# The second layer of a pair kernel in a written-out order, with the last chunk's banks and the last norm dealt out anew

## What is computed

```python
# layer one, per token (s, r)
x  = layernorm(pair) * ln1_w + ln1_b
left  = sigmoid(x @ left1) * (x @ left2)
right = sigmoid(x @ right1) * (x @ right2)
p  = layernorm(einsum('nsre,nkre->nske', left, right)) * ln2_w + ln2_b
x1 = pair + (p @ out_w) * sigmoid(x @ gate)
# layer two
l    = x1 @ (W_left + W_eq) + biases
rsum = sum of (x1 @ W_right + b_right) over one token axis
o    = l * rsum * sigmoid(x1 @ W_gate + b_gate)
out  = layernorm(o @ W_out + b_out + x1) * ln_scale + ln_bias
```

## Time and profile before

| what | before |
|---|---|
| median of three runs | 112.12 us |
| profiled execution | 112.37 us |
| its span, first to last instruction | 110.6 us |
| TensorE busy | 94.1 us (85%) |
| VectorE busy | 75.8 us (69%) |
| ScalarE busy | 66.4 us (60%) |
| GpSimd busy | 62.3 us (56%) |
| granted TensorE clock, mean | 0.968 |

### The profile page before, as it was taken

How to read it: one execution, slowest core, us unless ns; L and a number is a source line. 1 busy time by engine, 2 the same in 40 slices (tenths; PEclk the granted TensorE clock), 3 DMA queues, 4 the chain that set the end, 5 groups by cost and what they waited for, 6 DMA issues and landing times. The chain is left out here.

```text
span 110.6 us, 1889 instructions
## 1 busy us (share of the span) xinstructions
PE 94.1 (85%) x600; PEld 73.9 (67%) x600; DVE 75.8 (69%) x284; ACT 66.4 (60%) x110; POOL 62.3 (56%) x78
## 2 busy tenths in 40 slices
PE   1997889999999899999979999999999996499100
PEld 1994568667787899354536789777887885399000
DVE  1474799957879500989957599699789954983500
ACT  0633987977774366885699445982896499221000
POOL 5059954999910310055289595587865491799300
PEclk9999999999999999999999999999999999959985
DMA  3999990000000000000000000000032006029996
GB/s 59 190 152 143 147 134 21 0 0 0 0 0 3 6 0 0 0 0 3 0 0 0 9 0 0 0 0 6 0 55 40 0 0 95 0 41 146 145 146 101
DMA packets 33546, 4.54 MB, mean 41 GB/s; under 512 B 33408, under 2 KB 33536, under 8 KB 33536
## 3 DMA queue, kind: packets, MB, share of 16 engines
q1 hardware_dynamic: 31776, 4.03, 29.7%
q10 hardware_dynamic: 1760, 0.38, 1.8%
HBM read 2.31 MB, written 2.10 MB: 40 GB/s over the span
## 5 line engine op out<-in xcount | busy, mean ns | idle before, releaser
L596 DVE TENSOR_TENSOR lr<-bank,sig_lr 128x512 f32<-128x512 f32 x16 | 15.9, 1043 | 3.9 <-ACT sig_lr L431 3.9
L817 PE MATMUL bank<-lr_blk,xnT 64*128 64x256 f32 x128 | 16.5, 392 | 1.2 <-ACT xnT L421 0.7
L354 POOL TENSOR_TENSOR t_tok<-p_sb,rstd 128x512 f32<-128x512 f32 x7 | 10.2, 1461 | 11.8 <-DVE rstd L666 11.8
L362 POOL TENSOR_TENSOR x_low<-x1T,x_high 128x512 fp32r<-128x512 f32 x8 | 10.3, 1293 | 7.5 <-ACT x_high L501 7.5
L817 PEld LDWEIGHTS bank<-lr_blk,xnT 64*128 64x128 f32 x128 | 11.7, 186 | 4.2 <-issue 2.1
L660 DVE BATCH_NORM_STATS2 stats<-p_sb 128x6 f32<-128x64 f32 x64 | 8.5, 213 | 7.0 <-ACT p_sb L465 7.0
L370 POOL TENSOR_TENSOR oT<-o_a,rsum 128x512 f32<-128x512 f32 x8 | 8.7, 1088 | 6.4 <-DVE o_a L706 4.3
L431 ACT ACTIVATE sig_lr<-bank 128x512 f32<-128x512 f32 x16 | 9.6, 598 | 3.7 <-PE bank L817 3.6
L978 PE MATMUL bank<-wout_blk,oT 128*128 128x128 f32 x64 | 9.4, 293 | 2.2 <-POOL oT L370 2.2
L978 PEld LDWEIGHTS bank<-wout_blk,oT 128*128 128x128 f32 x64 | 8.5, 201 | 4.0 <-POOL oT L370 3.2
L501 ACT ACTIVATE x_high<-x1T 128x512 fp32r<-128x512 f32 x8 | 5.0, 626 | 8.5 <-DVE x1T L697 8.4
(11 more groups left out here) (104 smaller groups left out, 202.3 us busy)
## 6 DMA issues: line engine op xcount, KB each, us to landing
x_tok<-in_x SPq DMA_DIRECT2D x14, 128.0 KB, 4.2
out<-sq SPq DMA_DIRECT2D x7, 256.0 KB, 3.4
x_tok<-in_x SPq DMA_DIRECT2D x3, 64.0 KB, 3.0
w_rep<-in_weights ACTq DMA_DIRECT2D x4, 45.1 KB, 3.1
out<-sq ACTq DMA_DIRECT2D x1, 128.0 KB, 4.0
out<-sq SPq DMA_DIRECT2D x1, 128.0 KB, 4.5
x_tok<-in_x ACTq DMA_DIRECT2D x1, 64.0 KB, 2.7
row_rep<-in_rows SPq DMA_DIRECT2D x1, 32.0 KB, 4.2
```

The source lines that it names most:

```text
L354: nc.gpsimd.tensor_tensor(place(t_tok[:, c % 2], 0, SPC), even_first(p_sb[:, :, s]), even_first(rstd[:, 1:2, s]).to_broadcast([P, 2, SPC / ...
L362: nc.gpsimd.tensor_tensor(x1_low[:, c % 2], x1T[:, c % 3], x1_high[:, c % 2], ALU.subtract).then_inc(x1_low_ready, 1)
L596: nc.vector.tensor_tensor(lr[:, :, s].rearrange("p f s -> p s f"), src[:, :, 2 * CH:4 * CH], sig_lr[:, j % 3].rearrange("p (s f) -> p s f" ...
L817: last = nc.tensor.matmul(dst, xnT[half, c, k * P:(k + 1) * P], lr_blk[half].rearrange("p g m c -> p g (m c)"), start=True, stop=True, ski ...
```

## The change

Layer two is written out call by call on all four engines. Up to the fourth chunk the order is nearly that of the loops. Later chunks are interleaved more finely: the gate's and left side's matmuls are split into a part before and a part after `x1_low` is needed, `project_q`, `transpose_x` and `transpose_t` run ahead, and `residual0` is parted into `residual0` (`u`) and `add_x` (the four additions). Further:

- Chunks 0 and 7 are not split: `gate_whole` and `left_whole` are one float32 matmul each on `x1T`; `high1` and `low1` of the two go. Chunk 7 uses banks 0 and 1 for them, and its result and that of chunk 6 go to banks G and XT, so that `centre_y` of both needn't wait for the banks Y.
- `project_scaled`, `normalise3` and the scaled weights go. Chunks 6 and 7 take the way of the others.
- GpSimd makes `scale3` of 0, 1 and 4 and `bias3` of 0, 1, 4, 5, 6; VectorE `scale3` of 2, 3, 5, 6, `bias3` of 2 and 3, and all of chunk 7.
- The roots are taken in five groups, not six; stores are issued in the order 0, 2, 1, 3, 4, 5, 6.

```diff
-ROOTS3 = [(0, 1), (1, 3), (3, 5), (5, 6), (6, 7), (7, 8)]
+ROOTS3 = [(0, 1), (1, 3), (3, 6), (6, 7), (7, 8)]
+WHOLE = (0, 7)
+POOL_SCALES = [0, 1, 4]
+POOL_BIASES = [0, 1, 4, 5, 6]
+DVE_SCALES = [2, 3, 5, 6]
+DVE_BIASES = [2, 3]
+STORES = [0, 2, 1, 3, 4, 5, 6]
+        LAST_G, LAST_L = TT, Q
+        Y_BANK = [Y, Y + 1, Y, Y + 1, Y, Y + 1, XT, G]
...
 # GpSimd; before: times_right, low1, times_right, normalise2, bias3 by a loop
+            pool.wait_ge(r_in, 16)
+            normalise2(1); normalise2(2); normalise2(3); low1(1); normalise2(4)
+            times_right(0); low1(2); times_right(1); normalise2(5); low1(3)
+            normalise2(6); scale3(0); times_right(2); low1(4); bias3(0)
+            times_right(3); normalise2(7); low1(5); times_right(4)
+            scale3(1); bias3(1); low1(6); times_right(5); times_right(6)
+            scale3(4); bias3(4); times_right(7); bias3(5); bias3(6)
...
 # ScalarE, from the second root of layer two on
+            root2_of(3); root3_of(0); evacuate_y(1); evacuate_tT(5)
+            sigmoid_table(); gate1(3); high1(4); evacuate_tT(6); evacuate_y(2)
+            high1(5); gate1(4); root3_of(1); evacuate_y(3)
+            sigmoid_table(); gate1(5); evacuate_tT(7); high1(6); evacuate_y(4)
+            gate1(6); evacuate_y(5); root3_of(2)
+            sigmoid_table(); gate1(7); evacuate_y(6); root3_of(3)
+            evacuate_y(7); root3_of(4)
...
 # VectorE, from chunk 4 on
+            residual0(4); add_x(4); sums_of_right(1); residual0(5); gated1(3)
+            add_x(5); weigh3(1); variance3(1); weigh3(2); gated1(4)
+            variance3(2); sums_of_right(2); residual0(6); inverse3(1); add_x(6)
+            scale3(2); weigh3(3); bias3(2); gated1(5); weigh3(4); residual0(7)
+            variance3(3); variance3(4); add_x(7); gated1(6); sums_of_right(3)
+            variance3(5); inverse3(2); scale3(3); weigh3(5); bias3(3); gated1(7)
+            scale3(5); weigh3(6); variance3(6); inverse3(3); scale3(6)
+            variance3(7); weigh3(7); inverse3(4)
+            scale3_half(0); scale3_half(1); bias3_half(0); bias3_half(1)
...
 # TensorE, from chunk 4 on
+            transpose_x(4); project_sums(1); centre_y(2)
+            gate_high(3); left_high(3); gate_low(3); project_q(5); transpose_x(5)
+            left_low(3); transpose_t(6); project_y(2); gate_high(4); left_high(4)
+            transpose_x(6); gate_low(4); left_low(4); project_sums(2); centre_y(3)
+            project_q(6); project_y(3); left_high(5); transpose_t(7); gate_high(5)
+            gate_low(5); centre_y(4); project_y(4); left_low(5); project_q(7)
+            gate_high(6); transpose_x(7); centre_y(5); gate_low(6); project_y(5)
+            left_high(6); left_low(6); project_sums(3); centre_y(7); centre_y(6)
+            gate_whole(7); left_whole(7); project_y(6); project_y(7)
-            project_scaled(CHUNKS - 2)
-            project_scaled(CHUNKS - 1)
```

More of the change, by code:

```diff
@@ L373, in times_right, with scale3 @@
                                         ALU.mult).then_inc(oT_ready, 1)
+            def scale3(c):
+                s = slice(c * SPC, (c + 1) * SPC)
+                pool.wait_ge(rstd3, holding(ROOTS3, c) + 1)
+                pool.wait_ge(y_ready, c + 1)
+                nc.gpsimd.tensor_tensor(yn[:, s, :], y[:, s, :],
+                                        rstd[:, 2:3, s].rearrange("p a s -> p s a").to_broadcast([P, SPC, CH]),
+                                        ALU.mult).then_inc(pool_scaled, 1)
             def bias3(c):
                 s = slice(c * SPC, (c + 1) * SPC)
-                pool.wait_ge(scaled, c + 1)
+                if c in POOL_SCALES:
+                    pool.wait_ge(pool_scaled, POOL_SCALES.index(c) + 1)
+                else:
+                    pool.wait_ge(dve_scaled, DVE_SCALES.index(c) + 1)
                 nc.gpsimd.tensor_tensor(sq[:, s, :], yn[:, s, :], row_rep[:, 1:2, :].to_broadcast([P, SPC, CH]),
-                                        ALU.add).then_inc(final, 1)
+                                        ALU.add).then_inc(pool_final, 1)
+            pool.wait_ge(r_in, 16)
             normalise2(1)
[L383 to L395, removed]
+            normalise2(2)
+            normalise2(3)
+            low1(1)
+            normalise2(4)
+            times_right(0)
+            low1(2)
+            times_right(1)
+            normalise2(5)
+            low1(3)
+            normalise2(6)
+            scale3(0)
+            times_right(2)
+            low1(4)
+            bias3(0)
+            times_right(3)
+            normalise2(7)
+            low1(5)
+            times_right(4)
+            scale3(1)
+            bias3(1)
+            low1(6)
+            times_right(5)
+            times_right(6)
+            scale3(4)
+            bias3(4)
+            times_right(7)
+            bias3(5)
+            bias3(6)
         @block.scalar
@@ L554, in _, with sigmoid_table @@
-            for b in range(len(ROOT3_AT), len(ROOTS3)):
-                root3_of(b)
+            def sigmoid_table():
+                nc.scalar.activation(scratch[:], eps[:], ACT.Sigmoid)
+            evacuate_tT(0)
+            root2_of(1)
+            evacuate_tT(1)
+            root2_of(2)
+            evacuate_tT(2)
+            gate0(2)
+            gate0(3)
+            act.wait_ge(biases, 3)
+            high1(1)
+            gate1(0)
+            for c in range(4, CHUNKS):
+                gate0(c)
@@ new lines, in _ @@
+            evacuate_tT(3)
+            high1(2)
+            gate1(1)
+            evacuate_y(0)
+            evacuate_tT(4)
+            high1(3)
+            gate1(2)
+            root2_of(3)
+            root3_of(0)
+            evacuate_y(1)
+            evacuate_tT(5)
+            sigmoid_table()
+            gate1(3)
+            high1(4)
+            evacuate_tT(6)
+            evacuate_y(2)
+            high1(5)
+            gate1(4)
+            root3_of(1)
+            evacuate_y(3)
@@ L556, in _ @@
+            sigmoid_table()
+            gate1(5)
+            evacuate_tT(7)
+            high1(6)
+            evacuate_y(4)
+            gate1(6)
+            evacuate_y(5)
+            root3_of(2)
+            sigmoid_table()
+            gate1(7)
+            evacuate_y(6)
+            root3_of(3)
+            evacuate_y(7)
+            root3_of(4)
             s = slice(P - SPC, P - SPC // 2)
@@ L743, in _, with bias3_half @@
+            def bias3_half(h):
+                s = slice(P - SPC + h * SPC // 2, P - SPC + (h + 1) * SPC // 2)
+                dve.wait_ge(half_scaled, h + 1)
+                nc.vector.tensor_tensor(sq[:, s, :], yn[:, s, :], row_rep[:, 1:2, :].to_broadcast([P, SPC // 2, CH]),
+                                        ALU.add).then_inc(last_half, 1)
             dve.wait_ge(out0_ready, 2)
             dve.wait_ge(r_in, 16)
[L745 to L770, removed]
@@ L771, in _ @@
-            scale3(4)
+            statistics2(5)
+            residual0(0)
+            add_x(0)
+            inverse2(2)
+            residual0(1)
+            add_x(1)
+            gated1(0)
+            statistics2(6)
+            residual0(2)
+            sums_of_right(0)
+            add_x(2)
+            gated1(1)
+            statistics2(7)
+            residual0(3)
+            add_x(3)
+            weigh3(0)
+            variance3(0)
+            gated1(2)
+            inverse2(3)
+            inverse3(0)
@@ new lines, in _ @@
+            residual0(4)
+            add_x(4)
+            sums_of_right(1)
+            residual0(5)
+            gated1(3)
+            add_x(5)
+            weigh3(1)
+            variance3(1)
+            weigh3(2)
+            gated1(4)
+            variance3(2)
+            sums_of_right(2)
+            residual0(6)
+            inverse3(1)
+            add_x(6)
+            scale3(2)
+            weigh3(3)
+            bias3(2)
+            gated1(5)
+            weigh3(4)
+            residual0(7)
@@ L772, in _ @@
+            variance3(3)
+            variance3(4)
+            add_x(7)
+            gated1(6)
+            sums_of_right(3)
+            variance3(5)
+            inverse3(2)
+            scale3(3)
+            weigh3(5)
+            bias3(3)
+            gated1(7)
+            scale3(5)
+            weigh3(6)
             variance3(6)
-            scale3(5)
+            inverse3(3)
+            scale3(6)
+            variance3(7)
+            weigh3(7)
             inverse3(4)
-            variance3(7)
@@ L776, in _ @@
[L776 to L787, removed]
+            scale3_half(0)
@@ L980, in project_y @@
                 last.then_inc(y_ps, 1)
-            def project_scaled(c):
-                for n, (lhs, rhs) in enumerate(((x1T[:, c % 3], centre_scaled), (oT[:, c % 2], wout_scaled))):
-                    for j in range(BLK):
-                        k = slice(j * P, (j + 1) * P)
-                        last = nc.tensor.matmul(in_order(bank[:, SCALED + c % 2], j), lhs[:, k], rhs[:],
```

(63 more changed lines are left out.)

184 lines of the change are left out of this document (82 added, 102 removed).

## The result

The changed kernel takes 106.31 us (median of four runs, 106.10 to 107.79), the kernel before 112.12; the ratio is 0.946 (95% interval 0.944 to 0.948). Predicted were 107.0 us, 105.3 to 109.6. The profiled execution took 106.18 us, its span 104.4, 6.2 less than before.

The account below looks back on a forecast made before the run. Bound by compute until 104.2 us and 10.8 us of output transfer. Walks of the new end gave spans of 104.2 or 106.0; 105.5 was taken, plus 1.77, less 0.25 for the median: 107.0 us, range 105.3 to 109.6.

Parts of the forecast that it names:

- Two ends: End of the old kernel: set by compute until 104.2 us and by 10.8 us of output transfer until 109.7.
- Chunk 0: Start of layer two: unsplit, centre_y(0) begins at about 59.5 us, bound by ScalarE's gates; gain 0.6 us.
- The middle: Chunks 1 to 6 on TensorE: little gain; new waits of 0.3 us before transpose_x(6), 0 to 1.0 before project_y(5).
- the columns: Two walks of the kernel's end, without collisions and with every overlap waited out: span 104.2 or 106.0 us.
- The walk's steps: Predicted times at the kernel's end, from x1T(7) ready (87.9 or 89.35 us) to the last stores.
- The second column: Walk of the end with each VectorE and GpSimd overlap waited out: x1T(7) at 89.35, span 106.0 us.
- the free column: Walk of the end with no VectorE and GpSimd collision: x1T(7) at 87.9, last half 100.1, span 104.2 us.
- One sign of being wrong: At the last stores: DMA engines at 0.9 and more for 9 us up to the end would refute the prediction.
- The clock: Before project_y(7): if the granted clock falls to its half in the gap, it costs 0.75 us more.
- Stores still bunched: Rival at the last stores: chunk 3 leaves at 97.9 us and five chunks set the end; 110.4 us, chance 0.17.
- Slower by the clock in the middle: Rival in TensorE's full stretch: new waits drop the clock to half level; 114.2 us, chance 0.04.
- Free of collisions: Rival at the kernel's end: VectorE and GpSimd collisions have no weight; span 104.2, 105.7 us, chance 0.17.

Follow-up runs that it names:

- experiment 4: The changed kernel with chunk 0 split again (high1(0), low1(0), six matmuls): 106.75 us, +0.4.
- experiment 6: The changed kernel with VectorE's scale3 of chunks 3, 5, 6 and bias3 of 3 reading their first input from stale PSUM values: 105.57 us.
- experiment 8: The changed kernel with the third root earlier (gate_low(6), Sqrt's table load, variance3(5) and bias3(3) moved ahead): 106.98 us, +0.6.

## Why the prediction was right

**Two ends.** The reading that 10.8 us of transfer set the time, not the chain of waits, is shown from both sides: holding the stores brings the bunch back (+2.5), one bias moved in the old kernel takes 1.8 us off, and taking the chain's matmuls away takes nothing. (The row at 103.45 that the prediction calls VectorE's last instruction is its last two, one for each half; the end at 104.2 stands.)

**Chunk 0.** Forecast 0.6 us; measured 0.4 at the end and 0.5 at `centre_y(0)` (experiment 4), bound by the gates as said. Beside the kernel before, `centre_y(0)` is even 0.74 us earlier (59.39 for 60.13), but 0.26 of that stands ahead of chunk 0's matmuls (`project_q` at 53.44 for 53.70), and two profiles of the changed kernel differ there by as much (53.44 and 53.72).

**The middle.** Forecast of new waits: 0.3 before `transpose_x(6)` (0.40 measured) and 0 to 1.0 before `project_y(5)` (0 measured). `x1T(7)` was ready at 88.3; the columns had 87.9 and 89.35.

**The end.** The walk's steps, free / waits / measured: `gate1(7)` 92.0 / 93.4 / 92.3; `bias3(3)` 92.2 / 94.2 / 92.9; `gated1(7)` 93.0 / 94.9 / 93.6; GpSimd's `bias3(4)` 92.9 / 95.5 / 94.0; `times_right(7)` 94.1 / 97.15 / 95.5; `project_y(7)` 95.1 / 98.2 / 97.0; `bias3(6)` 98.5 / 100.35 / 98.6; last half 100.1 / 101.9 / 100.6; span 104.2 / 106.0 / 104.4. The order of the steps and the exclusion were right, and I leaned to the wrong column. Three sizes were wrong:

- GpSimd's `scale3` was taken at 1.3 us in three places; without a neighbour it takes 1.04, the lower bound.
- The second column had `x1T(7)` 1.45 us late for collisions in the middle; it was 0.4 late. From there to the last half the two columns need 12.2 and 12.55 us and the kernel took 12.3. So most of the 1.8 us between the columns lay ahead of `x1T(7)`.
- From the end of `project_y(7)` to that of `variance3(7)` the columns have 2.7 and 1.5 us. Measured are 1.4, and 1.5 in experiment 6, which is nearly the case free of collisions: the free column is 1.2 too long there, and from `x1T(7)` to the last half experiment 6 took 11.1 us for its 12.2. That its span of 104.2 comes so near to 104.4 is in part luck: `project_y(7)` ended 1.9 us after the free column's, and this error took nearly all of it up.

A collision itself costs what the second column charged. The five pairs of the rows above, the alone durations 0.68 us on VectorE, 1.04 (`scale3`, `times_right`) and 1.27 (`bias3`) on GpSimd:

| second to begin | begins | the first ends | left of the first | longer than alone |
|---|---|---|---|---|
| GpSimd `scale3(4)` | 90.78 | 91.43 | 0.65 | 0.51 |
| VectorE `bias3(3)` | 91.95 | 92.33 | 0.38 | 0.26 |
| GpSimd `bias3(4)` | 92.42 | 92.89 | 0.47 | 0.32 |
| VectorE `scale3(5)` | 93.47 | 94.01 | 0.54 | 0.41 |
| GpSimd `times_right(7)` | 93.97 | 94.56 | 0.59 | 0.45 |

Each time the extra is the first one's remainder less 0.12 to 0.15 us. The two VectorE products of experiment 8 follow it too: 0.78 and 0.88 us were left, 0.65 and 0.74 were added. The extras are small because little was left of the first, not because the two run side by side.

**The end of the stores.** GpSimd's last bias ended at 98.6 (the free column has 98.5), and the last of the data leaves at about 103.2 (103.3 there). One sign of being wrong came true all the same: the DMA engines were at 0.93 for 9.2 us up to the end. It was badly chosen, since five chunks need 9.0 us in any case and the prediction's own sum has them nearly without a gap; the pauses at 97 to 98 and 99 to 100 us show that the biases still set the pace, by little.

**The clock.** The granted clock fell to its half level (0.58 at 96 to 97 us, 0.50 behind it) after the gap of 2.29 us, as allowed for, and cost nothing, where the prediction would have had 0.75 us: in the profile with 2.07 us for `project_y(7)` VectorE ended at 101.2, 0.6 later, and the span was 104.5.

**Rivals.** Stores still bunched: no, first data at 93.9. Slower by the clock in the middle: no, 1.00 throughout 57.3 to 91.7. Free of collisions, 105.7: about as near in time (106.31 is 0.6 above it and 0.7 below the forecast), but wrong in its reason, as GpSimd's 1.55, 1.59, 1.49 show. The rule of the Trainium skill (SBUF — State Buffer, section Who interferes with whom) that the second of a pair waits is borne out by experiment 6 and by the table of pairs. The second column, which waits out every overlap, was 1.6 us too long for the moments that it read off its own late `x1T(7)`, not for that rule.

## What to carry to other kernels

Before working on the chain that ends last, divide the bytes still to be stored by the transfer rate and count back from the end: if that bunch reaches further back than the compute, what counts is when the first of its stores is released. Here 4.6 us of matmuls on the chain were worth nothing, and one elementwise instruction in an in-order queue 1.8 us. When two engines share elementwise work, place their two-input SBUF instructions beside the other's idle time or its PSUM work, and charge a collision with what is left of the first instruction when the second begins.

## Not expected of the hardware

On GpSimd, alone at their work and both 128 x 512 float32, an instruction whose second input repeats one value along the innermost dimension (`scale3`, `times_right`) took 1.04 us, and one whose second input is a row repeated from token to token (`bias3`) 1.27 (`normalise2`, with a second input of the first kind but a first input that is not contiguous, took 1.34); I had taken `scale3` for the second kind. The same kernel on the same inputs had `project_y(7)` at 1.25, 1.52 and 2.07 us in three executions, by when in it the granted clock fell.
